# A decoder layer on one core: plain fp32 matmuls in place of split ones, and down taken block by block

## The chip, the cores and the metric

One core of a Trainium2 (trn2) chip. The metric is the device time of one execution in microseconds, lower is better; the kernel before was timed in three runs.

## What is computed

A decoder layer in fp32: x has 4 batches of 1024 tokens of width 256. Three residual parts, each behind a layer norm: causal self-attention with 16 heads of 16, whose scores mix two bilinear forms that are folded into one query weight; cross-attention over 77 context tokens; and a gated feed-forward of 768 inner features. The change touches the first part's projections and the whole third part:

```
Q = LN(x) @ Wq.T + bq;  K = LN(x) @ Wk.T + bk;  V = LN(x) @ Wv.T + bv
...
gate = LN(x2) @ wg.T;  up = LN(x2) @ wu.T          # wg, wu: 768 x 256, int / 127
h    = silu(gate) * up
out  = x2 + h @ wd.T                               # wd: 256 x 768, int / 127
```

## The kernel before

Tokens are taken in eight chunks of 512 (`CH`), chunk c = 2b + u of batch b and half u; tiles with a dimension of 2 after the partitions alternate with u. `P` is 128, `KT` = 2 blocks of the width, `HT` = 6 blocks of the inner features, `J` = 4 blocks of 128 tokens in a chunk. Each engine has its own program, written out by hand, with counting semaphores between them; the order of the calls in `chunk` is that engine's order of work. `sweep` runs `chunk` over all eight, the first six in a loop. The stages follow one another:

- Opening: weights are loaded, turned on TensorE (L495) and emptied from PSUM by ScalarE (`empty`, L450) into `wk_t`, `wv_t`, `wo_t`, `wg_t`, `wu_t`, `wd_t`; the folded query weight goes into `wq_t`. For all but `wo_t` a second copy is made: ScalarE writes a reduced-precision value (type float32r), and VectorE's `low` (L388, 20 instructions) subtracts it from the bank and writes the remainder. A bank is free when both are done. Then the context's keys and values (L520, L527).
- QKV: per chunk TensorE multiplies for Q (two groups into banks 2, 3), turns the next chunk (`turn`, eight 128x128 transposes, L1218), multiplies for K (banks 4, 5) and then V (`values`, banks 6, 7). ScalarE copies the turned activations out (L1180) and VectorE subtracts to get their remainder (`turned_low`, L1111); ScalarE, VectorE (L1118) and GpSimd (L1156) split Q and K into three bf16 parts, which SyncE's queue stores. VectorE adds V's bias (L1138), normalises the next chunk (L221) and takes the moments of the one after.
- Self-attention, output projection with cross queries (L996, L1526), cross-attention: not edited. Their projections are plain fp32 matmuls: L1526 has a weight block stationary and 512 tokens moving, L996 and L1611 a block of 128 tokens stationary and 256 weight columns moving.
- Feed-forward, per chunk c on TensorE: the next chunk's cross output projection (`project3`, L1611, banks 0 and 1), gate and up for inner blocks 2, 3, 4, the next chunk's turn (L1794, banks 2 and 3), gate and up for block 5, then for blocks 0 and 1 of the next chunk, then `down` for all six blocks of chunk c into banks 0 and 1. Gate and up of block h go to banks 4 and 5 (h even) or 6 and 7 (h odd). ScalarE applies the gate's activation (L1768) and copies the turned chunk (L1762); VectorE multiplies (`hidden`, L1713), copies the product to float32r (L1715) and takes the remainder of the turned chunk (L1721); GpSimd takes the remainder of the product (`hidden_low`, L1684). VectorE also adds the projection to the residual (`sums3`, L1590), takes moments, normalises (L1601), and adds down's result to the residual (L1743), which SyncE stores.

Every product of QKV, gate, up and down is split: three matmul instructions (value by value, value by remainder, remainder by value; L184) into the same bank.

The semaphores around the change: `s_xt` says that a turned chunk may be multiplied, `s_gu` that a gate/up pair is in its banks, `s_h` that VectorE has multiplied a block, `s_y` that half of down's output is in its bank.

Of the kernel before, what the change touches and what calls it, by code (L numbers as in the profile page):

```python
# [29 lines left out]
F32R = mybir.dt.float32r  # L30
# [17 lines left out]
def program(nc, x, ctxt, mask, Wq, bq, Wk, bk, Wv, bv, Wo, bo, W_cross, shift_w, gate,  # L48
# [44 lines left out]
    with root:  # L93
# [29 lines left out]

        wq_t = sb("wq_t", [P, 2, KT, D], F32R)
        wk_t = sb("wk_t", [P, 2, KT, D], F32R)
        wv_t = sb("wv_t", [P, 2, KT, D], F32R)
# [6 lines left out]
        wg_t = sb("wg_t", [P, 2, KT, HID], F32R)  # L133
        wu_t = sb("wu_t", [P, 2, KT, HID], F32R)
        wd_t = sb("wd_t", [P, 2, HT, D], F32R)
# [97 lines left out]
        with ExitStack() as st:  # L233
# [38 lines left out]
            s_el = sem("w_el")  # L272
# [9 lines left out]
            def turned(src, dst, nk, no):  # L282
                for k in range(nk):
                    for o in range(0, no, 4):
                        n = min(4, no - o)
                        jobs.append(([src[:, o + i, k * P:(k + 1) * P] for i in range(n)],
                                     [d[:, k, o * P:(o + n) * P] for d in dst]))

            def both(w):
                return w[:, 0], w[:, 1]  # L290

            turned(n_k, both(wk_t), KT, KT)
            turned(n_v, both(wv_t), KT, KT)
            turned(n_o, (wo_t,), KT, KT)
            n_small = len(jobs)
            turned(fg, both(wg_t), KT, HT)
            turned(fu, both(wu_t), KT, HT)
            turned(fd, both(wd_t), HT, KT)
            NJ = len(jobs)
            cut = [n for n in range(NJ + KT) if n >= NJ or len(jobs[n][1]) == 2]  # L300
# [76 lines left out]
            def _(v):  # L377
                made = [0]

                def low(upto):  # L380
                    for n in cut[made[0]:upto]:
                        v.wait_ge(s_e, n + 1)
                        if n < NJ:
                            blocks, (hi, lo) = jobs[n]
                            w = len(blocks) * P
                        else:
                            hi, lo, w = wq_t[:, 0, n - NJ], wq_t[:, 1, n - NJ], D
                        nc.vector.tensor_tensor(lo, bank[n % NB][:, 0:w], hi.bitcast(F32), ALU.subtract).then_inc(s_el, 1)  # L388
                    made[0] = upto

# [36 lines left out]
                low(len(cut))  # L427
# [16 lines left out]
            def _(a):  # L444
# [7 lines left out]
                for n, (blocks, dst) in enumerate(jobs):  # L452
# [4 lines left out]
                    empty(n, dst[0], bank[n % NB][:, 0:len(blocks) * P])  # L457
                for k in range(KT):
                    empty(NJ + k, wq_t[:, 0, k, :], bank[(NJ + k) % NB][:, 0:D])
# [20 lines left out]
            def _(t_):  # L480
# [3 lines left out]
                def free(n):  # L484
                    if n >= NB:
                        t_.wait_ge(s_e, n - NB + 1)
                        if n - NB in cut:
                            t_.wait_ge(s_el, cut.index(n - NB) + 1)
# [28 lines left out]
                t_.wait_ge(s_el, len(cut))  # L517
# [494 lines left out]
        with ExitStack() as st:  # L1012
            scope[0] = st
            xnt = sb("a_xnt", [P, 2, 2, KT, CH], F32R)
# [4 lines left out]
            s_xh = sem("a_xh")  # L1019
# [84 lines left out]
            def _(v):  # L1104
                nc.vector.memset(vst[:].rearrange("p u g j h c -> p (u g j h) c")[:, :, HD:VW], 1.0)

                def turned_low(b, u):
                    c = 2 * b + u
                    for k in range(KT):
                        v.wait_ge(s_xh, 2 * c + k + 1)  # L1110
                        nc.vector.tensor_tensor(xnt[:, u, 1, k], bank[k][:], xnt[:, u, 0, k].bitcast(F32),  # L1111
                                                ALU.subtract).then_inc(s_xt, 1)

# [7 lines left out]
                def chunk(b, u, more):  # L1121
# [6 lines left out]
                    if more:  # L1128
# [733 lines left out]
```

## Time and profile before

| | us |
|---|---|
| runs of the kernel before | 1245.33, 1248.72, 1255.58 |
| median | 1248.72 |
| span of the profiled execution, first to last instruction | 1246.4 |
| TensorE busy in it | 1081.7 |
| TensorE's mean granted clock in it | 0.935 of full |

The profiled execution has no time of its own beside its span: the span runs from its first to its last instruction, and what lies around it isn't in the profile. In the page and the views, PE is TensorE's matmuls, PEld its weight loads (they overlap PE), DVE VectorE, ACT ScalarE, POOL GpSimd, SP or SPq SyncE's DMA queue. Matmuls are pipelined, so one record's duration is longer than the step from it to the next: a step is read from a group's start to the next group's start, or from the chain, not from a mean duration. L-numbers are lines of the kernel before. Float32r operands show as f32 in the shapes of matmuls.

### The profile page before, as it was taken

Reading aid. Unit: us, or ns where it says so; the run is one execution under the profiler, and the core shown is the slowest. Engines: PE = TensorE matmul, PEld = TensorE weight load, DVE = VectorE, ACT = ScalarE, POOL = GpSimd, SP = SyncE. Lnnn points to the kernel's source line nnn. Section 1 sums busy time; section 2 is a strip of 40 time slices with the busy share of each in tenths; the row PEclk is TensorE's granted clock in tenths of the full one; section 3 lists DMA queues with packets and bytes.
Section 4 is the critical chain, followed back from the end, with each engine's and each line's share of the span. In section 5 each row is a group of like instructions: output and inputs, shape, how many; then the busy total and the mean of one; then the engine's idle time right before and its main releaser. Section 6 shows DMA issues by size and latency. Waiting matters only on the chain. (4 is left out here: it accounts for less than half of the span.)

```text
span 1246.4 us, 23540 instructions
## 1 busy us (share of the span) xinstructions
PE 1081.7 (87%) x7116; PEld 640.1 (51%) x7164; DVE 792.2 (64%) x1705; ACT 557.3 (45%) x1022; POOL 216.0 (17%) x175
## 2 busy tenths in 40 slices
PE   1888969998999899999998665769999689999997
PEld 1677424443444344444443443434444278888886
DVE  4799837776777777777781775745555255555452
ACT  2456126665666666666666111216666321111110
POOL 4155510000000000000001233310000133333321
PEclk9899769998999989999999777859999889999999
DMA  6389892443344434444022578885666422222200
GB/s 196 104 289 309 252 149 70 85 91 71 75 86 87 87 69 86 86 87 90 18 74 87 170 218 234 245 235 148 173 177 163 148 68 68 68 67 67 67 18 34
DMA packets 132838, 153.30 MB, mean 123 GB/s; under 512 B 29003, under 2 KB 104319, under 8 KB 132735
## 3 DMA queue, kind: packets, MB, share of 16 engines
q1 hardware_dynamic: 126207, 145.74, 45.5%
q10 hardware_dynamic: 6528, 6.29, 1.5%
q8 instruction: 52, 0.85, 0.3%
q14 instruction: 51, 0.42, 0.1%
HBM read 87.69 MB, written 64.95 MB: 122 GB/s over the span
## 5 line engine op out<-in xcount | busy, mean ns | idle before, releaser
L687 DVE TENSOR_REDUCE self_pm<-bank 128x1 f32<-128x512 f32 (+3 forms) x608 | 365.4, 656 | 100.0 <-PE bank L772 68.7
L738 ACT ACTIVATE self_prob<-bank 128x512 f32<-128x512 f32 (+1 forms) x608 | 325.6, 577 | 184.1 <-PE bank L794 110.1
L786 PE MATMUL bank<-self_stq,self_stk 98*128 98x512 bf16 (+3 forms) x768 | 225.7, 334 | 24.9 <-DMA self_stq<-self_mrow 11.8
L763 PE MATMUL bank<-self_stk,self_stq 96*128 96x512 bf16 (+3 forms) x768 | 228.7, 342 | 8.1 <-DVE self_mrow L684 5.4
L806 PE MATMUL bank<-self_prob,self_va 128*32 128x512 f32 (+3 forms) x1536 | 163.7, 507 | 4.3
L763 PEld LDWEIGHTS bank<-self_stk,self_stq 96*128 96x128 bf16 x768 | 71.2, 100 | 162.4 <-DVE self_pm L687 111.8
L961 POOL TENSOR_TENSOR rin<-rin,bo_b 128x1024 f32<-128x1024 f32 x8 | 26.1, 3259 | 538.1 <-DMA min_<-mask_BxSxS_bk 538.1
L1768 ACT ACTIVATE e_sg<-bank 128x512 f32<-128x512 f32 x48 | 28.7, 599 | 191.9 <-PE bank L184 191.9
L786 PEld LDWEIGHTS bank<-self_stq,self_stk 98*128 98x128 bf16 x768 | 70.1, 99 | 83.8 <-issue 32.0
L738 ACT ACTIVATE cross_prob<-bank 96x512 f32<-96x512 f32 x128 | 74.8, 593 | 63.2 <-PE bank L791 63.0
L687 DVE TENSOR_REDUCE cross_pm<-bank 128x4 f32<-128x384 f32 x128 | 70.0, 557 | 35.0 <-PE bank L768 33.2
L996 PE MATMUL bank<-wo_t,oin 128*128 128x256 f32 x128 | 46.1, 537 | 41.7 <-DVE oin L919 36.4
L772 PE MATMUL bank<-tri_q,identb 128*128 128x128 bf16 (+2 forms) x333 | 81.3, 244 | 0.0
L184 PE MATMUL bank<-e_xnt,wg_t 128*128 128x512 f32 x288 | 78.4, 408 | 1.4 <-DVE e_xnt L1721 1.4
L794 PE MATMUL bank<-tri_k,identb 128*128 128x128 bf16 (+1 forms) x323 | 76.5, 237 | 0.0
L1684 POOL TENSOR_TENSOR e_ht<-e_hf,e_ht 128x512 fp32r<-128x512 f32 x48 | 62.6, 1303 | 76.8 <-DVE e_ht L1715 76.8
L184 PE MATMUL bank<-e_xnt,wu_t 128*128 128x512 f32 x288 | 75.6, 398 | 0.0
L184 PE MATMUL bank<-wd_t,e_ht 128*128 128x256 f32 x576 | 70.5, 282 | 3.2 <-POOL e_ht L1684 3.2
L184 PEld LDWEIGHTS bank<-wd_t,e_ht 128*128 128x128 f32 x576 | 70.1, 188 | 4.3 <-POOL e_ht L1684 3.7
L1713 DVE TENSOR_TENSOR e_hf<-bank,e_sg 128x512 f32<-128x512 f32 x48 | 33.1, 689 | 55.1 <-ACT e_sg L1768 42.9
L996 PEld LDWEIGHTS bank<-wo_t,oin 128*128 128x128 f32 x128 | 35.4, 284 | 54.6 <-issue 46.9
L184 PEld LDWEIGHTS bank<-e_xnt,wu_t 128*128 128x128 f32 x288 | 54.7, 190 | 13.4
(189 smaller groups left out, 1423.9 us busy)
## 6 DMA issues: line engine op xcount, KB each, us to landing
qk<-a_parts SPq DMA_DIRECT2D x32, 384.0 KB, 4.8
self_stq<-qk SPq DMA_DIRECT2D x192, 64.0 KB, 2.9
self_stk<-qk SPq DMA_DIRECT2D x96, 128.0 KB, 5.2
cross_stq<-xqs SPq DMA_DIRECT2D x32, 384.0 KB, 4.7
vs<-a_vst SPq DMA_DIRECT2D x8, 1024.0 KB, 5.5
self_va<-vs SPq DMA_DIRECT2D x16, 512.0 KB, 7.0
od<-self_u SPq DMA_DIRECT2D x16, 512.0 KB, 2.7
oin<-od SPq DMA_DIRECT2D x32, 256.0 KB
```

The lines of the kernel that those rows point to most:

```text
L184: mm = nc.tensor.matmul(dst, a[:, i], b[:, j], start=(n == 0), stop=(n == 3 * len(terms) - 1))
L687: nc.vector.tensor_reduce(pm[:, k, h0:h0 + hb, r], src[:, 0:hb * w].rearrange("p (h w) -> p h w", h=hb), AX, ALU.max).then_inc(s_mxe, 1)
L738: nc.scalar.activation(ops.prob[:, u % NPS, 0:hb * n], bank[ST_BANKS[u % 3]][0:KP, 0:hb * n], ACT.Exp).then_inc(s_ex, 1)
L763: mm = nc.tensor.matmul(dst[:, h * w:(h + 1) * w], stq[i][0:R, half, h0 + h, r * P:(r + 1) * P], stk[i][0:R, h0 + h, k0:k0 + w], start=(h ...
L772: mm = nc.tensor.matmul(dst[:, 0:hb * w].rearrange("p (h w) -> p h w", h=hb)[:, :, w - P:w], identb[:], tri_q[:, 0:hb], start=False, stop= ...
L786: mm = nc.tensor.matmul(dst[0:KP, h * n:(h + 1) * n], stk[i][0:RM, h0 + h, kt * KP:(kt + 1) * KP], stq[i][0:RM, half, h0 + h, q0:q0 + n], ...
L794: mm = nc.tensor.matmul(dst[:, 0:hb * n].rearrange("p (h n) -> p h n", h=hb)[:, :, 0:P], identb[:], tri_k[:, 0:hb], start=False, stop=True ...
L806: mm = nc.tensor.matmul(bank[PV_BANKS[half]][h * VW:(h + 1) * VW, q0:512], va[i][:, kt, h * VW:(h + 1) * VW], ops.prob[:, (first + h // hb ...
L996: mm = nc.tensor.matmul(bank[w][:, i * D:(i + 1) * D], oin[:, u, k, (2 * w + i) * P:(2 * w + i + 1) * P], wo_t[:, k], start=(k == 0), stop ...
L1684: nc.gpsimd.tensor_tensor(ht[:, u, 1, h], hf[:, h % 2], ht[:, u, 0, h].bitcast(F32), ALU.subtract).then_inc(s_hl, 1)
L1713: nc.vector.tensor_tensor(hf[:, h % 2], bank[5 + 2 * (h % 2)][:], sg[:, h % 2], ALU.mult).then_inc(s_h, 1)
L1768: nc.scalar.activation(sg[:, h % 2], bank[4 + 2 * (h % 2)][:], ACT.Silu).then_inc(s_sg, 1)
```

## The change

Both halves of it in words. First, the six split weight tiles, the turned activations `xnt` and the product `ht` become single fp32 tiles; `cut_products` with its three matmuls becomes `products` with one per pair; all instructions that made remainders (L388, L1111, L1721, L1684) and the copy L1715 are gone, with their semaphores. Second, in the feed-forward stage `down` is called per inner block, behind a wait for that block, and the order on TensorE becomes: projection, gate/up blocks 2 to 5, down blocks 0 to 3, the next chunk's turn, down blocks 4 and 5, gate/up blocks 0 and 1 of the next chunk. VectorE does the output additions (L1743) before `hidden` of the next chunk's blocks 0 and 1, where it did them after; ScalarE copies the turned chunk after all of this chunk's activations.

```diff
-        wq_t = sb("wq_t", [P, 2, KT, D], F32R)
+        wq_t = sb("wq_t", [P, KT, D])
...
-        def cut_products(dst, terms):
-            n = 0
-            for a, b in terms:
-                for i, j in ((0, 0), (0, 1), (1, 0)):
-                    mm = nc.tensor.matmul(dst, a[:, i], b[:, j], start=(n == 0), stop=(n == 3 * len(terms) - 1))
-                    n += 1
+        def products(dst, terms):
+            for n, (a, b) in enumerate(terms):
+                mm = nc.tensor.matmul(dst, a, b, start=(n == 0), stop=(n == len(terms) - 1))
             return mm
...
                 def hidden(b, u, h):
...
                     v.wait_ge(s_sg, 2 + HT * c + h + 1)
-                    v.wait_ge(s_hl, HT * c + h + 1)
-                    nc.vector.tensor_tensor(hf[:, h % 2], bank[5 + 2 * (h % 2)][:], sg[:, h % 2], ALU.mult).then_inc(s_h, 1)
-                    v.wait_ge(s_h, 2 + HT * c + h + 1)
-                    nc.vector.tensor_copy(ht[:, u, 0, h], hf[:, h % 2]).then_inc(s_hh, 1)
+                    nc.vector.tensor_tensor(ht[:, u, h], bank[5 + 2 * (h % 2)][:], sg[:, h % 2], ALU.mult).then_inc(s_h, 1)
...
-                    if more:
-                        turned_low(nb, nu)
                     hidden(b, u, 5)
-                    if more:
-                        hidden(nb, nu, 0)
-                        hidden(nb, nu, 1)
                     v.wait_ge(yd[u], 16 * (b + 1))
                     for w in range(2):
...
+                    if more:
+                        hidden(nb, nu, 0)
+                        hidden(nb, nu, 1)
...
-                def down(b, u, more):
-                    c = 2 * b + u
-                    t.wait_ge(s_hl, 2 + HT * (c + 1))
-                    if more:
-                        t.wait_ge(s_x2, 2 * (c + 1) + 2)
+                def down(b, u, h):
+                    c = 2 * b + u
+                    t.wait_ge(s_h, 2 + HT * c + h + 1)
                     for w in range(2):
                         for i in range(2):
                             tok = slice((2 * w + i) * P, (2 * w + i + 1) * P)
-                            mm = cut_products(bank[OB[w]][:, i * D:(i + 1) * D],
-                                              [(ht[:, u, :, h, tok], wd_t[:, :, h]) for h in range(HT)])
-                        mm.then_inc(s_y, 1)
+                            mm = nc.tensor.matmul(bank[OB[w]][:, i * D:(i + 1) * D], ht[:, u, h, tok], wd_t[:, h],
+                                                  start=(h == 0 and i == 0), stop=(h == HT - 1),
+                                                  skip_group_check=True)
+                        if h == HT - 1:
+                            mm.then_inc(s_y, 1)
 
                 def chunk(b, u, more):
+                    c = 2 * b + u
 
                     if more:
                         project3(t, b + u, 1 - u)
-                    for h in range(2, HT - 1):
+                    for h in range(2, HT):
                         gate_up(b, u, h)
                     if more:
+                        t.wait_ge(s_x2, 2 * (c + 1) + 2)
+                    for h in range(HT - 2):
+                        down(b, u, h)
+                    if more:
                         turn(b + u, 1 - u)
-                    gate_up(b, u, HT - 1)
+                    down(b, u, HT - 2)
+                    down(b, u, HT - 1)
                     if more:
                         gate_up(b + u, 1 - u, 0)
                         gate_up(b + u, 1 - u, 1)
-                    down(b, u, more)
```

## Rows read from the trace of the kernel before

**Rows 1.** The page's totals: busy us (share of the span) x instructions

```profile
PE 1081.7 (87%) x7116; PEld 640.1 (51%) x7164; DVE 792.2 (64%) x1705; ACT 557.3 (45%) x1022; POOL 216.0 (17%) x175
```

**Rows 2.** Busy time by stretch: us, engines (x), PEclk, DMA share, GB/s

```profile
core 0: us, PE busy (x) PEld busy (x) DVE busy (x) ACT busy (x) POOL busy (x), PEclk, DMA share, GB/s
46.90:134.30 87.40, 78.72 (x448) 67.16 (x448) 74.23 (x173) 48.89 (x80) 42.45 (x38) 0.96 0.93 272
134.30:998.80 864.50, 747.99 (x5248) 351.53 (x5296) 574.64 (x1203) 453.32 (x840) 74.60 (x44) 0.92 0.51 127
998.80:1246.40 247.60, 238.26 (x1328) 207.34 (x1328) 118.76 (x249) 38.09 (x65) 83.81 (x61) 0.98 0.20 57
...
93.50:104.20 10.70, 9.51 (x58) 8.12 (x57) 10.06 (x26) 6.11 (x11) 5.60 (x6) 1.00 0.97 270
```

**Rows 3.** The chain of waits, one feed-forward chunk: start us, us, what

```profile
1039.55 3.45 PE bank L1611 x16
1043.00 8.42 PE bank L184 x36
1051.42 0.87 PE bank L1794 x8
1052.30 17.06 PE bank L184 x108
```

**Rows 4.** Four lines' matmuls: duration ns min/median/max, first and last start, form

```profile
L184 PE MATMUL bank<-wd_t,e_ht x576: 278/282/384, 1030.7 to 1241.5; 128*128 128x256 f32 x192
...
L184 PE MATMUL bank<-e_xnt,wg_t x288: 388/397/796, 1002.2 to 1227.9; 128*128 128x512 f32 x144
...
L1526 PE MATMUL bank<-c_xnt,xwq x64: 592/592/697, 695.1 to 810.4; 128*128 128x512 f32 x64
...
L1611 PE MATMUL bank<-xwo,oin x128: 377/379/767, 984.9 to 1191.7; 128*128 128x256 f32 x128
```

**Rows 5.** TensorE's timeline at a plain 512-column group: start us, us, engine

```profile
695.08 3.69 PE L1526 MATMUL bank<-c_xnt,xwq 128*128 128x512 f32 x8 [0.66 <-ACT c_xnt L1483]
```

**Rows 6.** TensorE's timeline at the turn in one QKV chunk

```profile
97.63 1.09 PE L1218 MATMUL bank<-ident,a_xn 128*128 128x128 f32 x8 [1.19 <-DVE a_xn L221]
```

**Rows 7.** The timeline at the feed-forward stage's start and end

```profile
1000.86 0.60 ACT L1762 ACTIVATE e_xnt<-bank 128x512 fp32r<-128x512 f32 x1 [0.20 <-PE bank L1794]
...
1002.24 2.93 PE L184 MATMUL bank<-e_xnt,wg_t 128*128 128x512 f32 x6 [1.41 <-DVE e_xnt L1721]
...
1229.71 0.60 ACT L1768 ACTIVATE e_sg<-bank 128x512 f32<-128x512 f32 x1 [2.21 <-PE bank L184]
1230.34 0.69 DVE L1713 TENSOR_TENSOR e_hf<-bank,e_sg 128x512 f32<-128x512 f32 x1 [1.66 <-ACT e_sg L1768]
...
1232.88 8.89 PE L184 MATMUL bank<-wd_t,e_ht 128*128 128x256 f32 x72 [3.22 <-POOL e_ht L1684]
...
1241.82 0.69 DVE L1743 TENSOR_TENSOR e_yo<-bank,e_x 128x512 f32<-128x512 f32 x1 [3.56 <-PE bank L184]
```

**Rows 8.** Who waited for whom in QKV: us in total, times, longest

```profile
PE bank L1218 <- DVE a_xn L221: 7.1, 6, 1.2
```

**Rows 9.** VectorE's timeline over one QKV chunk

```profile
88.58 1.29 DVE L1111 TENSOR_TENSOR a_xnt<-bank,a_xnt 128x512 fp32r<-128x512 f32 x2 [0.53 <-ACT a_xnt L1180]
...
93.91 1.41 DVE L1138 TENSOR_TENSOR a_vst<-bank,bv_b 128x256 f32<-128x256 f32 x4
95.24 2.26 DVE L221 TENSOR_SCALAR a_xn<-a_xin,a_mom,a_rstd 128x256 f32<-128x256 f32 x4
```

**Rows 10.** The timeline in the opening, at L520

```profile
37.92 1.85 PEld L520 LDWEIGHTS bank<-c_t,xwk 128*128 128x128 f32 x8 [1.04 <-ACT c_t L450]
37.96 2.31 PE L520 MATMUL bank<-c_t,xwk 128*128 128x308 f32 x8 [0.92 <-DVE wq_t L388]
```

More of the change, by code:

```diff
@@ L29 @@
 F32 = mybir.dt.float32
-F32R = mybir.dt.float32r
 BF16 = mybir.dt.bfloat16
@@ L286, in turned @@
                         jobs.append(([src[:, o + i, k * P:(k + 1) * P] for i in range(n)],
[L287 to L294, printed above, removed]
+                                     dst[:, k, o * P:(o + n) * P]))
+            turned(n_k, wk_t, KT, KT)
+            turned(n_v, wv_t, KT, KT)
+            turned(n_o, wo_t, KT, KT)
             n_small = len(jobs)
-            turned(fg, both(wg_t), KT, HT)
-            turned(fu, both(wu_t), KT, HT)
-            turned(fd, both(wd_t), HT, KT)
+            turned(fg, wg_t, KT, HT)
+            turned(fu, wu_t, KT, HT)
+            turned(fd, wd_t, HT, KT)
             NJ = len(jobs)
-            cut = [n for n in range(NJ + KT) if n >= NJ or len(jobs[n][1]) == 2]
             N_FOLD = NJ + KT
@@ L377, in _ @@
             def _(v):
[L378 to L389, printed above, removed]
                 v.wait_ge(s_in, 16 * N_IN)
@@ L456, in _ @@
                             nc.scalar.activation(f[:], i[:], ACT.Identity, scale=WSCALE).then_inc(s_f, 1)
-                    empty(n, dst[0], bank[n % NB][:, 0:len(blocks) * P])
+                    empty(n, dst, bank[n % NB][:, 0:len(blocks) * P])
                 for k in range(KT):
-                    empty(NJ + k, wq_t[:, 0, k, :], bank[(NJ + k) % NB][:, 0:D])
+                    empty(NJ + k, wq_t[:, k, :], bank[(NJ + k) % NB][:, 0:D])
                 empty(N_FOLD, qkb[:, 0, :], bank[N_FOLD % NB][:, 0:KT])
@@ L1179, in turned @@
                         a.wait_ge(s_tr, 4 + 2 * c + k + 1)
-                        nc.scalar.activation(xnt[:, u, 0, k], bank[k][:], ACT.Identity).then_inc(s_xh, 1)
+                        nc.scalar.activation(xnt[:, u, k], bank[k][:], ACT.Identity).then_inc(s_xt, 1)
                 def high(b, u, n):
@@ L1226, in values @@
                         tok = slice((2 * w + i) * P, (2 * w + i + 1) * P)
-                        m = cut_products(bank[VB[w]][:, i * D:(i + 1) * D],
-                                         [(xnt[:, u, :, k, tok], wv_t[:, :, k]) for k in range(KT)])
+                        m = products(bank[VB[w]][:, i * D:(i + 1) * D],
+                                     [(xnt[:, u, k, tok], wv_t[:, k]) for k in range(KT)])
                     m.then_inc(s_vm, 1)
@@ L1236, in chunk @@
                         w_ = (wq_t, wk_t)[n // 2]
-                        m = cut_products(bank[QKB[n]][:],
-                                         [(w_[:, :, k, (n % 2) * P:(n % 2 + 1) * P], xnt[:, u, :, k]) for k in range(KT)])
+                        m = products(bank[QKB[n]][:],
+                                     [(w_[:, k, (n % 2) * P:(n % 2 + 1) * P], xnt[:, u, k]) for k in range(KT)])
                         m.then_inc(s_qk, 1)
@@ L1761, in turned @@
                         a.wait_ge(s_tr, 4 + 2 * c + k + 1)
-                        nc.scalar.activation(xnt[:, u, 0, k], bank[TB[k]][:], ACT.Identity).then_inc(s_xh, 1)
+                        nc.scalar.activation(xnt[:, u, k], bank[TB[k]][:], ACT.Identity).then_inc(s_xt, 1)
                 def silu(b, u, h):
@@ L1774, in chunk @@
                         turned(b + u, 1 - u)
-                    silu(b, u, HT - 1)
-                    if more:
                         silu(b + u, 1 - u, 0)
@@ L1803, in gate_up @@
                     for w_, o in ((wg_t, 4), (wu_t, 5)):
-                        mm = cut_products(bank[o + 2 * (h % 2)][:],
-                                          [(w_[:, :, k, h * P:(h + 1) * P], xnt[:, u, :, k]) for k in range(KT)])
+                        mm = products(bank[o + 2 * (h % 2)][:],
+                                      [(w_[:, k, h * P:(h + 1) * P], xnt[:, u, k]) for k in range(KT)])
                     mm.then_inc(s_gu, 1)
-                def down(b, u, more):
+                def down(b, u, h):
                     c = 2 * b + u
-                    t.wait_ge(s_hl, 2 + HT * (c + 1))
-                    if more:
-                        t.wait_ge(s_x2, 2 * (c + 1) + 2)
+                    t.wait_ge(s_h, 2 + HT * c + h + 1)
                     for w in range(2):
```

58 lines of the change are left out of this document (10 added, 48 removed).

## The prediction

> **What bounds the kernel now.** I read first the page's totals: TensorE is busy for 87% of the span and VectorE for 64% [rows 1]. That is a mean over stages, so next came busy time by stage: the change touches the opening, the QKV stage (46.9 to 134.3 us) and the feed-forward stage (998.8 to the end), and the 864 us of attention between them aren't edited [rows 2]. In the feed-forward stage TensorE is busy 238.3 of 247.6 us, VectorE 118.8, GpSimd 83.8. The chain of waits names what is late there: four pieces of TensorE work repeat without a gap, 3.45 us of projection, 8.42 us for 36 split products' matmuls, 0.87 us of turning and 17.06 us for 108, which makes 29.8 us for a chunk [rows 3]. So this stage is TensorE's alone, and nothing that the change takes from VectorE or GpSimd is on its path, except at its two ends. In QKV both are full: in one chunk of 10.7 us TensorE is busy 9.51 and VectorE 10.06 [rows 2], TensorE's timeline has one gap per chunk, 1.19 us before the turn [rows 6], and the waits put six such gaps, 7.1 us in all, to VectorE's normalisation at L221 [rows 8].
>
> **Price of one product.** A product is one pair of 128-row operands added into a bank. Split, it is three matmul instructions; the 36 of the chain take 8.42 us, 0.234 us each, 0.702 us per product of 512 columns [rows 3]. The piece of 108 is 36 such and the 72 of down; 17.06 - 8.42 = 8.64, over 72 0.120 us, so 0.360 us per product of 256 columns.
> Plain, the trace already has both shapes. L1526 (weights stationary, 512 tokens moving, as gate, up, Q and K will be) is 8 chunks x 2 x 2 = 32 products and shows 64 records: two per product [rows 4]. Its eight records of one chunk take 3.69 us; the last one lasts 0.592 us by itself, so 7 steps take 3.10 and one takes 0.443, a product 0.885 us [rows 4, 5]. L1611 (tokens stationary, 256 weights moving, as V and down will be) has 128 records for 64 products, and its 16 take 3.45 us on the chain, 0.431 us per product [rows 3, 4]. So a plain product costs 0.885 - 0.702 = 0.183 us more at 512 columns and 0.431 - 0.360 = 0.071 us more at 256. Bounds: if the 512-column record had no more than twice the 256-column record's 0.2156 us, a product would be 0.862; and nothing that switches banks oftener than L1611 (every second product; down now at each one) is in the trace, for which I allow 0.01 us a product either way.
>
> The Trainium skill, "FP8 and Floating Point Precision", section "TensorE Precision Notes", says that true fp32 makes four passes through the array. If each of them cost what one split matmul does, a product would be 4 x 0.234 = 0.936 and 4 x 0.120 = 0.480 us; the records of rows 3 to 5 say 0.885 and 0.431, so two passes seem to share one record's fixed part, and the sum goes by the records. The dearer reading is a rival below.
>
> **Feed-forward, eight chunks.** Gate and up: 6 x 2 x 2 = 24 products a chunk, 192 in all, x 0.183 = +35.2 us. Down: 4 x 6 = 24 a chunk, 192, x 0.071 = +13.7. Together +48.9, all of it on the path: a chunk becomes 29.8 + 6.1 = 35.9 us. What leaves elsewhere (VectorE's copy L1715 and subtraction L1721, GpSimd's L1684) was beside TensorE and gives nothing in the middle.
> Down's reordering adds a wait for the multiplied block before each of six blocks. Behind such a wait stand TensorE's later products, and everyone waits for these. The tightest is block 5: after the last up product come the sigmoid-gated activation (0.60 us) and the multiplication (0.69) [rows 7], some 1.4 us with their hand-overs, against blocks 0 to 4 of down, 20 products or 8.6 us. Five waits out of six are for work long done. Each gate/up pair already has such a wait and its pieces run without a gap, so a wait that is met costs nothing I can see; the upper bound, were block 5's to come first, is 1.4 us a chunk.
> The turn of the next chunk moves behind four blocks of down. Its two copies on ScalarE (0.60 us each [rows 7]) must end before the next gate product; blocks 4 and 5 cover them with 3.45 us. If that cover were gone, 1.3 us a chunk would show. What the turn itself waits for, VectorE's normalisation, gets some 11 us more room. On VectorE the output additions (L1743) now stand ahead of the next chunk's blocks 0 and 1. They wait for down's end, after which TensorE has two gate/up pairs (7.1 us) and then the projection (3.4) before it needs block 0: additions 2 x 0.7 [rows 7], activation and multiplication fit. The projection needs the additions, which end 0.9 us after down, and is 7.1 us off. SyncE stores the output after the same additions, with a chunk's time to do it; GpSimd's quotients only come earlier.
> At the ends: at the start TensorE waits 1.41 us for copy and subtraction; the copy alone ends at 1001.46, and the first product could begin at 1001.5 in place of 1002.24: -0.7. At the end it waits 3.22 us for the chain activation, multiplication, copy, GpSimd; now four blocks of down stand there: -3.2 [rows 7]. The granted clock is below full only near the stage's start, and I take the time lost there as unchanged (bounds -1.5 to +1.5).
>
> **QKV, eight chunks.** Q and K: 4 x 2 = 8 products a chunk, 64 in all, x 0.183 = +11.7. V: 64 x 0.071 = +4.5. Together +16.2 of TensorE time. VectorE loses two subtractions a chunk, 1.3 us, which with its 0.53 us wait before them [rows 9] leaves some 8.9 us of work per chunk against TensorE's 8 x 0.885 + 8 x 0.431 + 0.87 = 11.4. So TensorE alone becomes the bound. What is next late is the turn again: it follows two groups of the new chunk, 3.54 us after the values end, where it was 2.8. VectorE then has the last two value additions (0.7 us, 0.2 of hand-over) and the normalisation, 2.26 us when GpSimd runs beside it [rows 9]: ready 3.2 us after, 0.3 before it's needed. So I let the 7.1 us of gaps go wholly, and keep 0 to 7.1 for the range. The first chunk's wait loses its subtractions too: -0.7. ScalarE's copies for the turn and its first splits fit inside 11.4 us (it was busy 6.1 a chunk [rows 2]); the stores are the same bytes over a longer chunk.
>
> **Opening.** VectorE's 20 subtractions leave. Only one wait of TensorE named them: 0.92 us before L520 [rows 10]; its weight load waited for ScalarE until nearly the same moment, so I take -0.2 (bounds 0 and -0.9).
>
> **Sum.** 48.9 + 16.2 - 7.1 - 0.7 - 0.7 - 3.2 - 0.2 = +53.2 us. The profiled execution's span is 1246.4 us, 2.3 below the median of 1248.72 and inside the runs' spread; its changed span would be 1299.6, and the median 1302.
>
> **Rivals.**
> A, the forecast: 1302, chance 0.79. Its own bounds: the cheaper 512-column product (256 x 0.023 = -6), the bank switches (2 to 4 either way), and the spread of the runs.
> B, VectorE's normalisation stays late in QKV. Its distance of 0.3 us is small, and if VectorE drags the whole 1.19 along, the 7.1 us are not won: 1309. Against it: 1.3 us less work per chunk ahead of it. Chance 0.11. A cover lost in feed-forward (1.3 us x 7) would come out alike.
> C, each plain record takes the time of two split matmuls, a product so 4 x 0.234 and 4 x 0.120: 256 x (0.936 - 0.702) + 256 x (0.480 - 0.360) = +90.6, less the same 11.9: 1327. Only the lone groups of L1526 speak for the smaller number at 512 columns; L1611 speaks against it inside the dense stage. Chance 0.04. This is the skill's four passes at the split record's price.
> D, the other side: the spacing at L1526 is that of a lone group with its loads, and in a dense stream each record takes what a split matmul does, 0.234 and 0.120. A product is then 0.468 and 0.240, TensorE loses 256 x 0.234 + 256 x 0.120 = 90.6 us, of which QKV, then bound by VectorE at 8.9 us a chunk, gives about 13 of its 22.7, and the kernel ends near 1248.7 - 68 - 13 - 5 = 1163. It decides from where the plain price falls by 16% (0.745 and 0.363 us), when the sum is nothing. For it: two records against three. Against it: L1526's records last 0.592 us against 0.397 for a split one of the same columns, and L1611's 0.431 is taken inside the dense stage itself. Chance 0.03.
> E, no more than 1% either way, by D's mechanism halfway: 0.03.
>
> **The numbers.** Time 1302. Low end 1289: the cheaper product, switches that cost less and the spread; high end 1313: B with the spread. C, D, E and the edges are left out, about 0.14. A measurement of this kernel tells about 1% from no change. Slower by over 1% are A, B and C, 0.94; within 1% E, 0.03; faster D, 0.03.
>
> **What would show it.** A feed-forward chunk on the chain should be 35.9 us, with gate/up pieces of about 0.885 us a product, down 0.431, and TensorE 100% busy; no 3.2 us wait near the end. QKV's chunk should be 11.4 us with no gap at the turn (11.4 + 1.2 = 12.6 would be B), its end at about 143. Plain records at 0.234 us spacing would make it wrong altogether; so would a gap before a down block or before the first gate product of a chunk. The stages between should keep their 864 us.

## The result, and the profile after

The changed kernel takes 1296.24 us (median of four runs, 1290.49 to 1296.61) against 1250.61 in the runs of before beside it: a ratio of 1.0369 with a 95% interval of 1.0323 to 1.0416, slower by 45.6 us. The forecast was 1302 and +53.2. The profiled spans are 1294.8 and 1246.4 us, 48.4 apart.

The page's totals of the changed kernel, busy us, share of the span and instructions, where rows 1 stood before:

```profile
PE 1141.3 (88%) x6652; PEld 595.3 (46%) x6652; DVE 737.6 (57%) x1605; ACT 556.9 (43%) x1022; POOL 152.3 (12%) x127
```

TensorE's busy time rose by 59.6 us, VectorE's fell by 54.6 and GpSimd's by 63.7 [rows 1]; the time went the way of TensorE's. By stretch (us, then each engine's busy time and count, granted clock, DMA share, GB/s), where rows 2 stood before; the last two are one QKV chunk and one feed-forward chunk:

```profile
core 0: us, PE busy (x) PEld busy (x) DVE busy (x) ACT busy (x) POOL busy (x), PEclk, DMA share, GB/s
142.00:1007.10 865.10, 747.85 (x5296) 348.41 (x5294) 573.19 (x1203) 453.37 (x840) 73.70 (x43) 0.92 0.50 125
1007.10:1294.80 287.70, 282.71 (x944) 175.41 (x944) 88.85 (x185) 38.76 (x65) 20.97 (x13) 0.99 0.17 49
101.00:112.20 11.20, 11.20 (x42) 6.91 (x41) 7.91 (x23) 5.91 (x10) 5.52 (x5) 1.00 1.21 249
1058.00:1093.30 35.30, 35.30 (x122) 22.12 (x121) 11.86 (x25) 4.67 (x8) 3.33 (x2) 1.00 0.22 60
```

In QKV VectorE is now busy 7.91 of 11.20 us, where it was 10.06 of 10.70 [rows 2], and TensorE all of it. Between the ends of the feed-forward stage TensorE was and is busy all the time. The chain of waits of the changed kernel over one feed-forward chunk, start us, us and what, answers to rows 3:

```profile
1054.70 3.45 PE bank L1567 x16
1058.15 13.73 PE bank L179 x32
1071.89 6.91 PE bank L1739 x32
1078.79 0.87 PE bank L1719 x8
1079.67 3.46 PE bank L1739 x16
1083.12 6.87 PE bank L179 x16
```

Projection 3.45, gate and up of blocks 2 to 5 13.73, four blocks of down 6.91, the turn 0.87, two blocks of down 3.46, gate and up of blocks 0 and 1 6.87: 35.3 us and not a gap, against 29.8. Where the 48.4 us stand, read at the same four events in both traces:

| stretch | before | after | measured | forecast |
|---|---|---|---|---|
| start to QKV's first turn | 46.95 | 47.67 | +0.7 | -0.2 |
| QKV's first turn to self-attention's first matmul | 87.60 | 94.18 | +6.6 | +8.4 |
| from there to feed-forward's first turn | 864.34 | 865.28 | +0.9 | 0 |
| feed-forward's first turn to the last addition's start | 242.93 | 283.44 | +40.5 | +45.0 |
| the rest | 4.58 | 4.23 | -0.3 | 0 |

The stretch in the middle was not edited. In the ten traces of this document it lasts from 859.1 to 865.3 us, so a difference of a few us between two whole executions can come from there.

TensorE's timeline of the changed kernel over one QKV chunk, where rows 6 stood before:

```profile
86.33 3.60 PE L179 MATMUL bank<-a_xnt,wq_t 128*128 128x512 f32 x8
89.76 1.04 PE L1177 MATMUL bank<-ident,a_xn 128*128 128x128 f32 x8
90.63 3.60 PE L179 MATMUL bank<-a_xnt,wk_t 128*128 128x512 f32 x8
94.07 3.62 PE L179 MATMUL bank<-wv_t,a_xnt 128*128 128x256 f32 x16
97.52 3.60 PE L179 MATMUL bank<-a_xnt,wq_t 128*128 128x512 f32 x8
```

The turn follows without a gap; the chunk, from one first Q product to the next, is 11.19 us where it was 10.75.

### The profile page after: what moved, and what is told of

The parts are those of the page before. It is cut to its first block and busy times, and to the rows that moved or that the text cites. A ratio compares the mean times of both kernels' runs of the same rounds, so it can differ in the third digit from the quotient of the medians.

```text
span 1294.8 us, 22329 instructions
## 1 busy us (share of the span) xinstructions
PE 1141.3 (88%) x6652; PEld 595.3 (46%) x6652; DVE 737.6 (57%) x1605; ACT 556.9 (43%) x1022; POOL 152.3 (12%) x127
## 5 line engine op out<-in xcount | busy, mean ns | idle before, releaser
L1652 DVE TENSOR_TENSOR e_ht<-bank,e_sg 128x512 f32<-128x512 f32 x48 | 33.2, 691 | 109.3 <-ACT e_sg L1695 109.3
L179 PE MATMUL bank<-e_xnt,wg_t 128*128 128x512 f32 x192 | 92.1, 603 | 0.7 <-ACT e_xnt L1689 0.7
L179 PE MATMUL bank<-e_xnt,wu_t 128*128 128x512 f32 x192 | 91.0, 596 | 0.0
L742 PE MATMUL bank<-tri_q,identb 128*128 128x128 bf16 (+2 forms) x352 | 89.0, 253 | 0.0
L764 PE MATMUL bank<-tri_k,identb 128*128 128x128 bf16 (+2 forms) x352 | 87.7, 249 | 0.0
L1739 PE MATMUL bank<-wd_t,e_ht 128*128 128x256 f32 x384 | 85.3, 379 | 0.0
L966 PE MATMUL bank<-wo_t,oin 128*128 128x256 f32 x128 | 42.3, 502 | 42.4 <-DVE oin L889 37.1
L179 PEld LDWEIGHTS bank<-e_xnt,wu_t 128*128 128x128 f32 x192 | 36.9, 192 | 47.0 <-issue 47.0
L966 PEld LDWEIGHTS bank<-wo_t,oin 128*128 128x128 f32 x128 | 32.7, 262 | 54.2 <-issue 47.5
L776 PEld LDWEIGHTS bank<-self_prob,self_va 128*32 128x32 f32 x1536 | 32.2, 109 | 54.9 <-issue 28.0
```

Source lines behind the costliest of these rows:

```text
L179: mm = nc.tensor.matmul(dst, a, b, start=(n == 0), stop=(n == len(terms) - 1))
L742: mm = nc.tensor.matmul(dst[:, 0:hb * w].rearrange("p (h w) -> p h w", h=hb)[:, :, w - P:w], identb[:], tri_q[:, 0:hb], start=False, stop= ...
L764: mm = nc.tensor.matmul(dst[:, 0:hb * n].rearrange("p (h n) -> p h n", h=hb)[:, :, 0:P], identb[:], tri_k[:, 0:hb], start=False, stop=True ...
L776: mm = nc.tensor.matmul(bank[PV_BANKS[half]][h * VW:(h + 1) * VW, q0:512], va[i][:, kt, h * VW:(h + 1) * VW], ops.prob[:, (first + h // hb ...
L966: mm = nc.tensor.matmul(bank[w][:, i * D:(i + 1) * D], oin[:, u, k, (2 * w + i) * P:(2 * w + i + 1) * P], wo_t[:, k], start=(k == 0), stop ...
L1652: nc.vector.tensor_tensor(ht[:, u, h], bank[5 + 2 * (h % 2)][:], sg[:, h % 2], ALU.mult).then_inc(s_h, 1)
```

## The experiments

Eight kernels ran besides the changed one, each timed in rounds beside the kernel before.

**e1: plain products in QKV alone.**

```diff
 (kernel before)
-        wq_t = sb("wq_t", [P, 2, KT, D], F32R)
+        wq_t = sb("wq_t", [P, KT, D])
...
-                        m = cut_products(bank[QKB[n]][:],
-                                         [(w_[:, :, k, (n % 2) * P:(n % 2 + 1) * P], xnt[:, u, :, k]) for k in range(KT)])
+                        m = products(bank[QKB[n]][:],
+                                     [(w_[:, k, (n % 2) * P:(n % 2 + 1) * P], xnt[:, u, k]) for k in range(KT)])
...
-                    if more:
-                        turned_low(nb, nu)
```

> The kernel before with plain products in QKV alone; feed-forward stays split and in the old order. Theory (TensorE's steps alone set both stages; a plain product of 512 columns costs 0.859 us, of 256 0.432, against 0.702 and 0.360): a QKV chunk of 11.2 us without a gap at the turn against 10.75 with one, the stage some 6.6 us longer, the feed-forward stage unchanged at 242.9 us from its first turn to its last addition, the whole +7 us. Rival (the gap of 1.19 us per chunk stays, VectorE's normalisation being late as before): a chunk of 12.4 us, the whole +14. Rival (the time is paid in feed-forward's reordering, not in the products): QKV unchanged, the whole within 2 us.

Measured: 1257.33 us, ratio 1.0088 (1.0057 to 1.0118). TensorE's timeline of one QKV chunk of e1:

```profile
84.94 3.60 PE L180 MATMUL bank<-a_xnt,wq_t 128*128 128x512 f32 x8
88.37 1.04 PE L1210 MATMUL bank<-ident,a_xn 128*128 128x128 f32 x8
...
96.13 3.60 PE L180 MATMUL bank<-a_xnt,wq_t 128*128 128x512 f32 x8
```

Chunks of 11.19 us and no gap, as the theory said; the rival with the gap kept (12.4) falls, and so does the one that put all of the price in feed-forward. From the first turn to self-attention's first matmul it is 93.4 us, +5.8. The whole came out some 3 us dearer than expected (by the interval +7 to +15 us), and in the profile 2.9 us stand in the feed-forward stage, which was not edited (245.8 us against 242.9). 2.4 of them are in its last down. The clock by stretch of e1 there:

```profile
core 0: us, PE busy (x) PEld busy (x) DVE busy (x) ACT busy (x) POOL busy (x), PEclk, DMA share, GB/s
...
1238.40:1243.00 4.60, 4.51 (x21) 4.51 (x22) 0.00 (x0) 0.00 (x0) 0.04 (x1) 0.50 0.00 0
1243.00:1250.00 7.00, 6.82 (x53) 6.61 (x52) 0.83 (x2) 0.00 (x0) 0.00 (x0) 0.92 0.00 0
```

TensorE had stood still for 3.2 us before it, as in the kernel before; here it then ran at half its clock for some 4.6 us (0.50 granted, the 1.2 GHz level), and the last down took 11.35 us where the chain of before shows 8.91. Four traces have this wait: before, e1, e5 and e6. Only in e1's did the clock fall behind it (e5's down took 8.89 us), so the wait can cost more than its length, and no run here tells when it does.

**e2: the changed kernel with feed-forward in the old order.**

```diff
 (changed kernel)
-                    for h in range(2, HT):
+                    for h in range(2, HT - 1):
                         gate_up(b, u, h)
-                    if more:
-                        t.wait_ge(s_x2, 2 * (c + 1) + 2)
-                    for h in range(HT - 2):
-                        down(b, u, h)
                     if more:
                         turn(b + u, 1 - u)
-                    down(b, u, HT - 2)
-                    down(b, u, HT - 1)
+                    gate_up(b, u, HT - 1)
                     if more:
                         gate_up(b + u, 1 - u, 0)
                         gate_up(b + u, 1 - u, 1)
+                    down(b, u, more)
```

> The changed kernel with feed-forward put back into the old order: down whole, behind block 5 and the next chunk's blocks 0 and 1. Theory (the order gives nothing between the chunks, only cover at the end): chunks of 35.3 us as in the changed kernel, and one wait before the last down for activation and multiplication, 1.4 us; the whole +1.4. Rival (a bank switched at every down product costs TensorE some 0.01 us each): chunks of 35.0 us, the whole -1 or faster. Rival (the order hides more than the end, the turn's copies above all): a gap per chunk at the next chunk's first gate product, the whole +8 or more.

Measured: 1296.15 us, ratio 1.0402 (1.037 to 1.0434); the changed kernel had 1.0369. The chain of e2 over one chunk:

```profile
1050.62 3.45 PE bank L1567 x16
...
1065.25 20.66 PE bank L179 x72
1085.91 3.45 PE bank L1567 x16
```

Again 35.3 us (1050.62 to 1085.91) without a gap: neither the place of output, which in the changed kernel is another half of a bank at every product of down, nor the moved turn costs or gives anything. At the end TensorE waits 1.41 us for activation and multiplication:

```profile
1277.50 10.63 PE L179 MATMUL bank<-wd_t,e_ht 128*128 128x256 f32 x48 [1.41 <-DVE e_ht L1652]
```

The stage is 284.8 us from its first turn to its last addition against 283.4. The new order is worth 1.3 us to the plain kernel (1.7 at its end, of which 0.4 is hidden here by a start that happened to be quicker: 9.29 us for the first 16 records against 9.66), and at its end alone; between whole kernels that is less than the runs tell.

**e3: the new order alone, with split products.**

```diff
 (kernel before)
-                    t.wait_ge(s_hl, 2 + HT * (c + 1))
+                    t.wait_ge(s_hl, 2 + HT * c + h + 1)     # in down(b, u, h), called for each block
...
                     hidden(b, u, 5)
                     if more:
-                        hidden(nb, nu, 0)
-                        hidden(nb, nu, 1)
+                        turned_low(nb, nu)
```

> The kernel before with the new order of feed-forward alone, all products still split, with all of VectorE's and GpSimd's work. Theory: chunks of 29.8 us as before, the wait of 3.2 us before the last down gone, the whole -3. Rival (the order needs the lighter VectorE and GpSimd of the plain kernel): gaps on TensorE before down blocks or before the next chunk's first gate product, chunks over 30.5 us, the whole +3 or more.

Measured: 1242.92 us, ratio 0.997 (0.9954 to 0.9986), 3.9 us faster. The chain of e3 over one chunk and the start of its last down:

```profile
1040.00 3.45 PE bank L1613 x16
...
1069.81 3.45 PE bank L1613 x16
...
1230.09 7.93 PE bank L1815 x66
```

A chunk is 29.8 us (1040.00 to 1069.81) as before, and the last down follows its gate and up at once. The order does not need the lighter engines. So of the two halves of the change the order is a small gain by itself, and with e1 and e2 it is the plain products that make the kernel slower.

**e4: VectorE's and GpSimd's work put back.** Two instructions per block write tiles that nothing reads.

```diff
 (changed kernel)
                     nc.vector.tensor_tensor(ht[:, u, h], bank[5 + 2 * (h % 2)][:], sg[:, h % 2], ALU.mult).then_inc(s_h, 1)
+                    v.wait_ge(s_h, 2 + HT * c + h + 1)
+                    v.wait_ge(s_hv, HT * c + h + 1)
+                    nc.vector.tensor_copy(hv[:, h % 2], ht[:, u, h]).then_inc(s_hv, 1)
...
+                    nc.gpsimd.tensor_tensor(hg[:, h % 2], ht[:, u, h], ht[:, u, h], ALU.subtract).then_inc(s_echo, 1)
```

> The changed kernel with VectorE's copy of 0.43 us and GpSimd's subtraction of 1.3 us put back for each of the 48 blocks, into tiles that nothing reads. Theory (TensorE alone bounds the stage, what was taken from the two engines was worth nothing): chunks of 35.3 us, the whole within 1 us of the changed kernel. Rival (their release had given back part of the price, through shared SBUF or late operands): chunks over 35.6 us, the whole +3 or more.

Measured: 1294.14 us, ratio 1.0379 (1.035 to 1.0408), which can't be told from the changed kernel's 1.0369. The chain of e4, the projection that opens one chunk and the next:

```profile
1052.89 3.45 PE bank L1569 x16
...
1088.18 3.45 PE bank L1569 x16
```

The chunk is 35.3 us with the work and without it, the stage 283.6 against 283.4. So the copy and the subtraction that the change took from the two engines for each block were worth nothing. VectorE's other subtraction (L1721, two per chunk) was not put back; in e3, which has all of this work, a chunk has no gap either.

**e5: could the kernel before have won QKV's gap by order?**

```diff
 (kernel before, VectorE's QKV chunk)
-                    if more:
-                        normalise1(v, nb, nu)
                     split(b, u, 0)
...
                     split(b, u, 3)
+                    if again(b):
+                        normalise1(v, b + 1, u)
                     v.wait_ge(vo[u], 16 * (b + 1))
```

> The kernel before with VectorE's normalisation in QKV moved ahead of the value additions and done two chunks ahead, so that TensorE's turn finds it ready. Theory (the gap of 1.19 us came from VectorE's order, but VectorE has only 0.6 us of slack in a chunk of 10.7): the gap at the turn goes, a chunk falls to some 10.1 us, the whole -4. Rival (the gap was a matter of order alone): chunks of 9.6 us, the whole -7. Rival (something else holds the turn, such as ScalarE's copies): no change.

Measured: 1252.14 us, ratio 1.0045 (1.0026 to 1.0064): a miss, slower. VectorE's and GpSimd's rows of the timeline of e5 around one turn, and TensorE's turn:

```profile
83.88 3.06 DVE L221 TENSOR_SCALAR a_xn<-a_xin,a_mom,a_rstd 128x256 f32<-128x256 f32 x4
84.05 2.43 POOL L1157 TENSOR_TENSOR a_parts<-a_rest,a_parts 128x512 bf16<-128x512 f32 x2 [0.33 <-ACT a_parts L1190]
...
87.08 1.09 PE L1219 MATMUL bank<-ident,a_xn 128*128 128x128 f32 x8 [1.53 <-DVE a_xn L221]
```

By the chunk's index the normalisation is two ahead, but in time it only moved ahead of four value additions, from 1.76 us behind the chunk's first Q product (95.24 [rows 9], with that product at 93.48) to 1.28 (83.88, with it at 82.60). And there it meets two of GpSimd's subtractions (84.05 on), and its four instructions take 3.06 us where they took 2.26 [rows 9]. Behind the chunk's first Q product it ends at 4.34 us where it ended at 4.02, the gap grows from 1.19 to 1.53 us, and a chunk is 11.09 us. The same line's durations, min/median/max in ns, between 60 and 125 us, first in the kernel before:

```profile
L221 DVE TENSOR_SCALAR a_xn<-a_xin,a_mom,a_rstd x24: 398/401/1296, 63.0 to 118.6; 128x256 f32<-128x256 f32 x24
```

and in e5:

```profile
L221 DVE TENSOR_SCALAR a_xn<-a_xin,a_mom,a_rstd x24: 400/822/1268, 61.7 to 119.8; 128x256 f32<-128x256 f32 x24
```

The shortest and the longest are alike, the median doubled: before, one of a chunk's four instructions stood beside one of GpSimd's and took 1.28 to 1.30 us; in e5 two do and take 1.24 to 1.27, and the others 0.40. Each long one ends some 0.15 us behind the end of the GpSimd instruction beside it. The Trainium skill, "SBUF — State Buffer", section "SBUF: two separate sides", says that VectorE, in a two-port mode or with two inputs in SBUF, and GpSimd take a shared pair of ports in turn, each for a whole instruction, the other blocked. The traces fit that; whether L221 runs in such a mode they don't show.

The gaps are the smaller part of what e5 lost in QKV. TensorE's first rows of self-attention, in the kernel before and in e5:

```profile
134.55 0.84 PE L763 MATMUL bank<-self_stk,self_stq 96*128 96x128 bf16 x6 [0.28 <-DMA self_va<-vs]
```

```profile
139.87 0.61 PE L763 MATMUL bank<-self_stk,self_stq 96*128 96x128 bf16 x4 [4.37 <-DMA self_va<-vs]
```

By the last chunk's first Q product e5 is 1.2 us behind (126.86 against 125.63), by self-attention's first matmul 5.3: the other 4.1 us are a wait for the load of V, which SyncE's queue issued at 131.63 in place of 129.00 and which landed 8.2 us later in place of 5.5. e7, with the same edit, shows the same wait (4.45 us), e8 without it 0.81. Behind the wait TensorE's granted clock was 0.50 for at least 5 us, where it was 1.00 in the kernel before. What made the load late was not taken apart. Nor is it shown how much of this reaches the whole: the profiled execution of e5 was the fastest of ten, its span is 1246.4 us like that of before, and its attention stretch was 5.3 us shorter. The medians differ by 5.5 us.

**e6: fewer split products by exact weights.** If TensorE's steps are the price, the way down is fewer of them. Gate, up and down weights are integers times 1/127. Kept as integers they have no remainder, the third matmul of each product goes, and the factors move into the activation and the last addition.

```diff
 (kernel before)
-        wg_t = sb("wg_t", [P, 2, KT, HID], F32R)
+        wg_t = sb("wg_t", [P, KT, HID], F32R)
...
-                        mm = cut_products(bank[o + 2 * (h % 2)][:],
-                                          [(w_[:, :, k, h * P:(h + 1) * P], xnt[:, u, :, k]) for k in range(KT)])
+                        for n in range(2 * KT):
+                            mm = nc.tensor.matmul(bank[o + 2 * (h % 2)][:], w_[:, n // 2, h * P:(h + 1) * P],
+                                                  xnt[:, u, n % 2, n // 2], start=(n == 0), stop=(n == 2 * KT - 1))
...
-                    nc.scalar.activation(sg[:, h % 2], bank[4 + 2 * (h % 2)][:], ACT.Silu).then_inc(s_sg, 1)
+                    nc.scalar.activation(sg[:, h % 2], bank[4 + 2 * (h % 2)][:], ACT.Silu, scale=WSCALE).then_inc(s_sg, 1)
...
+                        nc.vector.scalar_tensor_tensor(..., bank[OB[w]][:], WSCALE * WSCALE, ..., ALU.mult, ALU.add)
```

> The kernel before in its old order, with gate, up and down weights kept as the integers they are (the factor 1/127 goes to the activation and, squared, to the last addition), so that they have no remainder and a product takes two split matmuls. Theory (a product costs what its steps cost, 2 x 0.234 and 2 x 0.120 us): 192 x 0.234 + 192 x 0.120 = 68 us less on TensorE, but gate and up pairs now come every 1.9 us where VectorE has 1.1 us for each block and its sums, moments and normalisation besides, so some gaps of 2 to 3 us per chunk appear: chunks of 23 to 24.5 us against 29.8, the whole -43 to -55. Rival (TensorE alone still bounds): chunks of 21.3 us, the whole -68.

Measured: 1200.09 us, ratio 0.9629 (0.958 to 0.9678), 46.5 us faster. TensorE's timeline of e6 around its gaps:

```profile
1053.27 3.62 PE L1611 MATMUL bank<-xwo,oin 128*128 128x256 f32 x16
...
1063.68 1.09 PE L1795 MATMUL bank<-ident,e_xn 128*128 128x128 f32 x8 [0.81 <-DVE e_xn L1601]
...
1067.67 1.19 PE L1806 MATMUL bank<-e_xnt,wg_t 128*128 128x512 f32 x4 [1.03 <-DVE e_xnt L1721]
```

The chain of e6 before one down:

```profile
1043.27 2.35 POOL oin L919
...
1045.99 1.30 POOL e_ht L1684
...
1047.42 6.02 PE bank L1819 x48
```

A chunk is 24.4 us (1029.04 to 1053.43 on its chain), 3.1 over what TensorE's own steps make (24 x 0.468 + 24 x 0.240 + 3.45 + 0.87 = 21.3). TensorE's two large gaps, 0.81 and 1.03 us, name VectorE at L1601 and L1721. But down waits for all six blocks, and the chain to it runs over GpSimd: its quotients for the next batch (L919, 2.35 us) stand between its remainders of the product (L1684, 1.3 us each). So both engines are late here, and closing the two gaps would not by itself bring down forward. Chunk and whole lie where the theory had them (23 to 24.5, -43 to -55), though it named VectorE alone, and the rival of 21.3 falls.

**e7: e6 with the changed kernel's order and e5's normalisation.** The two diffs above on top of e6.

> Two matmuls per product as in e6, with the changed kernel's order of feed-forward and e5's normalisation. Theory: the turn behind four blocks of down gives VectorE more room, so chunks fall to 21.5 to 23 us, with no wait at the end; the whole -60 to -75, some 1180 us, and faster than both kernels. Rival (VectorE bounds whatever the order): chunks as in e6, the whole -50.

Measured: 1192.22 us, ratio 0.9564 (0.9521 to 0.9607): 54.4 us faster, short of the 60 to 75 of the theory and near the rival's 50. VectorE's timeline of e7:

```profile
1062.79 0.43 DVE L1718 CAST e_ht<-e_hf 128x512 fp32r<-128x512 f32 x1
1063.29 2.42 DVE L1604 TENSOR_SCALAR e_xn<-e_x,e_mom,e_rstd 128x256 f32<-128x256 f32 x4
1065.63 0.68 DVE L1716 TENSOR_TENSOR e_hf<-bank,e_sg 128x512 f32<-128x512 f32 x1
```

The normalisation (2.42 us) stands between the multiplications of blocks 2 and 3, and TensorE's gate and up of block 5, which needs block 3's bank, waits 1.41 us for it: chunks of 23.35 us, over the 21.5 to 23 expected. GpSimd's remainders are off the chain here: down goes block by block, and the remainder of block 5 stands ahead of the quotients. And e5's edit in QKV is itself a loss in that stage: from the first turn to self-attention's first matmul e7 takes 93.2 us where e6 took 88.8.

**e8: the normalisation behind block 4, QKV as before.**

```diff
 (e7, VectorE's feed-forward chunk)
                     hidden(b, u, 2)
-                    if more:
-                        normalise3(v, nb, nu)
                     hidden(b, u, 3)
                     hidden(b, u, 4)
+                    if more:
+                        normalise3(v, nb, nu)
                     hidden(b, u, 5)
```

> The kernel of e7 with QKV as in the kernel before, and feed-forward's normalisation of the next chunk moved behind the multiplication of block 4. In e7 a chunk took 23.35 us with one gap of 1.41 us and a late pair of gate and up, both behind that normalisation, which stood between blocks 2 and 3. Theory (with the normalisation out of the way of the blocks TensorE alone bounds the stage): chunks of 21.5 us, the whole some 14 us under e7 for this and 3 to 5 more for QKV: 1172 to 1178. Rival (the gap moves to the turn or to down's block 5, since VectorE still has the same work): chunks over 22.5 us, the whole over 1182.

Measured: 1177.54 us (1176.48 to 1180.56), ratio 0.9428 (0.9399 to 0.9456), faster than both kernels. One feed-forward chunk of e8 in busy time by stretch:

```profile
core 0: us, PE busy (x) PEld busy (x) DVE busy (x) ACT busy (x) POOL busy (x), PEclk, DMA share, GB/s
1052.50:1074.20 21.70, 21.61 (x121) 18.64 (x121) 15.20 (x34) 4.68 (x8) 11.23 (x8) 1.00 0.36 97
```

TensorE is busy 21.61 of 21.70 us with VectorE at 15.20: the stage is TensorE's again but for 0.4 us over its own steps of 21.3, at 21.7 us a chunk where it was 29.8. Chunk and whole (1172 to 1178) are the theory's. e8 differs from e7 in two things; by stage, feed-forward is 11.1 us shorter (173.8 against 184.9) and QKV with the start of attention 4.5 (88.8 against 93.2), while the unedited attention stretch is 3.7 longer in this trace.

## Why the prediction was right, point by point

**The bound.** Right. TensorE alone set the feed-forward stage: between its chunks there is no gap in either kernel, and e4 shows that the work taken from VectorE and GpSimd for each block gave nothing.

**The 256-column product.** Right: 6.91 us for 16 products of down is 0.432 us, forecast 0.431. That down changes its place of output at every product costs nothing (e2), where I had allowed 0.01 either way. (What changes at every product is the half of a bank; the bank itself changes at every second, where L1611's changes at every fourth.)

**The 512-column product: mis-sized.** I priced it at 0.885 us; the chain shows 13.73 us for 16, 0.858. The step that failed is the reading of the eight records at L1526: I took 3.69 less the last record's 0.592 as seven equal steps. In the changed kernel the same line still shows 3.69, after a wait, while eight such records in a full stream take 3.60 us (the QKV rows above), which is seven steps of 0.429. The missing 0.09 belongs to the first record after a wait, not to the step. The trace of before had it: the group starts at 695.08, and the weight loads that go with its next records stand at

```profile
695.61 0.19 PEld L1526 LDWEIGHTS bank<-c_xnt,xwq 128*128 128x128 f32 x1 [0.24 <-issue]
696.04 0.19 PEld L1526 LDWEIGHTS bank<-c_xnt,xwq 128*128 128x128 f32 x1 [0.24 <-issue]
```

so the first step is 0.53 us and the next 0.43. The longest record of rows 4, 697 ns where 592 is the median, pointed the same way. TensorE's timeline of the changed kernel at that line:

```profile
704.12 3.69 PE L1485 MATMUL bank<-c_xnt,xwq 128*128 128x512 f32 x8 [0.66 <-ACT c_xnt L1442]
```

Over 256 products that is 256 x 0.027 = 6.9 us too dear; without it the forecast (1.037) lies inside the measured interval, with it (1.0426) just above. The lower bound I had given (twice the 256-column record, 0.862) was the true value to 0.004. At a granted clock of 1.00, the 2.4 GHz level, 0.858 us are 2059 cycles, 4.02 for each of the 512 columns. The Trainium skill, "FP8 and Floating Point Precision", section "TensorE Precision Notes", has four passes for true fp32; the 4.02 agree with that if a pass takes a column per cycle. Priced by the split matmul's 0.234 four would have come out at 0.936.

**QKV.** Right in kind: TensorE became the bound and the gaps went (the changed kernel and e1). The chunk was forecast at 11.4 and is 11.2. That the stretch came out so near, +6.6 against +8.4, is partly luck. The mis-sized product is 64 x 0.027 = 1.7 of the difference, and three other terms cancel. First, six gaps gave 8.2 us and not 7.1: a gap is counted from the end of the last record, some 0.16 us behind its step, so each cost 1.36 us (a chunk of 10.73 to 10.75 less TensorE's 24 x 0.234 + 24 x 0.120 + 0.87 = 9.4). Second and third, the clock in the first chunk, which I had left out. TensorE's rows at the stage's start, before:

```profile
46.95 1.94 PE L1218 MATMUL bank<-ident,a_xn 128*128 128x128 f32 x8 [3.23 <-SPq L1041]
50.38 4.46 PE L184 MATMUL bank<-a_xnt,wq_t 128*128 128x512 f32 x12 [1.49 <-DVE a_xnt L1111]
```

and in the changed kernel:

```profile
47.67 1.06 PE L1177 MATMUL bank<-ident,a_xn 128*128 128x128 f32 x8 [3.22 <-SPq L1010]
49.62 6.71 PE L179 MATMUL bank<-a_xnt,wq_t 128*128 128x512 f32 x8 [0.89 <-ACT a_xnt L1139]
```

The first turn ran at half clock before and at full clock here, 0.9 us won; the first chunk's Q lost 3.1 us to the half clock here (6.55 us to the next turn in place of 3.43) and 1.5 before (4.30 in place of 2.81), 1.6 us lost. The wait behind the first turn fell by 0.6, forecast 0.7. With these 16.2 - 1.7 - 8.2 - 0.9 + 1.6 - 0.6 = 6.4 us of the 6.6.

My margin of 0.3 us for the normalisation was wrong on the safe side. The changed kernel's normalisation and the turn behind it:

```profile
109.59 1.37 DVE L213 TENSOR_SCALAR a_xn<-a_xin,a_mom,a_rstd 128x256 f32<-128x256 f32 x4
```

```profile
112.15 1.04 PE L1177 MATMUL bank<-ident,a_xn 128*128 128x128 f32 x8
```

It is ready 1.2 us before the turn. I had given it 2.26 us, beside GpSimd; here no GpSimd instruction stands beside it.

**Down's waits and the moved turn.** Right: no gap before any block, none before the next chunk's gate, with plain products (changed kernel) and with split ones (e3). The room that the turn gains is 12.2 us on the chain (20.64 between projection and turn in place of 8.42), and 12.6 by my own prices, not the 11 that I wrote.

**The ends.** Right at the end of the stage: -3.2. That is the price of the wait of the kernel before; e2 and e3 part it. With split products the order removes it; with plain ones and the old order 1.41 would be left. At the start TensorE's wait behind the turn fell from 1.41 to 0.69 us, forecast -0.7.

**The clock at the stage's start.** I took it as unchanged, with 1.5 us either way. From the first gate product to the projection (1009.75 to 1019.25) the first 16 records of feed-forward took 9.50 us where they take 6.87 at full clock, 2.6 us lost; before, the first 24 took 7.32 (1002.24 to 1009.56) where they take 5.61, 1.7 lost. So 0.9 more, inside the bound. The granted clock of these first microseconds was 0.58 here and 0.60 before.

**Sum.** With 0.858 in place of 0.885 my sum is 53.2 - 6.9 = +46.3; the spans differ by 48.4 and the medians by 45.6. Of the spans' remaining 2.1 us, 0.9 stand in the opening, 0.9 in the attention stretch and 0.7 in feed-forward, where the clock lost 0.9; QKV has -0.1 and the rest -0.3. In the opening the wait before L520 fell from 0.92 to 0.57 us, as I had it; that QKV began 0.7 us later all the same is scatter of the execution (e2 and e4, with the same opening, begin at 47.10 and 46.98).

**Rivals.** B (the gap stays): not seen. C and D (four or two split matmuls' time a product, 0.936 or 0.468): the product is 0.858. E (within 1%): outside the interval of 1.0323 to 1.0416.

## What to carry to other kernels

A stage that one engine fills can be forecast as its step times the number of steps, and what the other engines lose is worth nothing except at the stage's ends. Take a step from a full stream, or from a start to the next group's start: a group behind a wait gives its first record's latency to the steps. To make such a stage faster, ask which operands are exact: weights that are small integers need no remainder, and two matmuls per product in place of three, with VectorE's long instructions out of the way of the short ones that free banks, took 5.7% off this kernel (e8) where plain fp32 added 3.7%. And before moving an instruction of VectorE, look which of GpSimd's it will then stand beside, and what the stage hands on at its end: in e5 the end of the stage cost more than all the gaps.

## What the runs showed of the hardware that I had not expected

The same wait of 3.2 us before the last down left TensorE's clock at full in the profile of before (the down behind it took 8.91 us) and at half for 4.6 us in e1's (11.35 us); e5's and e6's traces show it at full.

The steps of split and plain matmuls are not in the ratio of their passes, with one for a split matmul. A split matmul of 512 columns takes 0.234 us in a full stream, a plain record 0.429, which is 0.214 a pass if a product has four and a record holds two of them; at 256 columns 0.120 and 0.108. The plain product therefore costs 1.22 times the split one of three matmuls (0.858 to 0.702), not 4/3. No run here tells why a split matmul takes a tenth more than a pass.

VectorE's normalisation instruction of 0.40 us took 1.24 to 1.30 beside one of GpSimd's, so that moving the four of a chunk half a microsecond earlier, where two of them met GpSimd in place of one, made them end later (e5).
